# Edge counting in a graph network kernel: one-hot rows built as a product of two small one-hots, edge columns innermost

## The reference

```python
def step(h, _):
    messages = h[col] @ W_msg.T + b_msg                       # col = dst
    agg = jax.ops.segment_sum(messages, row, num_segments=num_nodes)   # row = src
    gi = agg @ W_ih.T + b_ih
    gh = h @ W_hh.T + b_hh
    r = sigmoid(i_r + h_r); z = sigmoid(i_z + h_z)
    n = tanh(i_n + r * h_n)
    return (1.0 - z) * n + z * h, None
h, _ = jax.lax.scan(step, x, None, length=5)
x = _layernorm(x + h)
```

## Time and profile before

| | us |
|---|---|
| median of 3 runs | 702.73 (701.65 to 703.63) |
| the profiled execution | 700.98 |
| its span, first to last instruction | 699.0 |

### The profile page before, as it was taken

How to read it: one execution, slowest core, us unless ns; L and a number is a source line. 1 busy time by engine, 2 the same in 40 slices (tenths; PEclk the granted TensorE clock), 3 DMA queues, 4 the chain that set the end, 5 groups by cost and what they waited for, 6 DMA issues and landing times.

```text
span 699.0 us, 8918 instructions
## 1 busy us (share of the span) xinstructions
PE 633.2 (91%) x3065; PEld 476.3 (68%) x3065; DVE 383.1 (55%) x1043; ACT 324.0 (46%) x557; POOL 261.3 (37%) x348
## 2 busy tenths in 40 slices
PE   3569888888899999999999999989999989999992
PEld 3445555555585587788778877867888868778861
DVE  4699999999966742332642223561332453244446
ACT  3446666666643443444444334433443443344342
POOL 6000000000012056566446655535676536556610
PEclk9579999999999999999999999999999999999997
DMA  5023333333300000000000000000000000000002
GB/s 162 23 59 83 83 87 89 87 87 87 86 25 0 0 1 1 0 1 0 1 1 1 0 1 0 1 0 1 1 0 1 1 0 1 1 0 1 0 21 74
DMA packets 37710, 18.71 MB, mean 27 GB/s; under 512 B 4588, under 2 KB 37482, under 8 KB 37662
## 3 DMA queue, kind: packets, MB, share of 16 engines
q1 hardware_dynamic: 35304, 16.70, 9.2%
q0 software_dynamic: 416, 0.83, 0.4%
q10 hardware_dynamic: 1942, 0.55, 0.3%
HBM read 2.96 MB, written 1.60 MB: 7 GB/s over the span
## 4 chain that ended last, share of the span: by engine, by line
PE 66%; DVE 28%; ACT 3%; issue 2%; DMA 1%; POOL 0%; DVEq 0%; ACTq 0%
PE PS L665 37%; DVE hot_row L1083 15%; PE PS L645 8%; PE PS L646 8%; DVE hot_key L1078 6%; PE PS L653 4%; PE PS L652 4%; PE PS L516 3%; PE PS L588 2%; ACT ring L872 1%; DVE parts L970 1%; DVE hT L1127 1%; DVE pre_n L1123 1%; DVE pre_n L1111 1%; ACT cand L865 1%
## 5 line engine op out<-in xcount | busy, mean ns | idle before, releaser
L480 POOL CAST ring<-A 128x896 fp32r<-128x896 uint8 (+4 forms) x324 | 249.9, 810 | 399.3 <-PE PS L665 207.9
L665 PE MATMUL PS<-ring,parts 128*128 128x448 f32 x1372 | 301.4, 374 | 1.9 <-ACT ring L872 1.9
L665 PEld LDWEIGHTS PS<-ring,parts 128*128 128x128 f32 x1372 | 254.3, 188 | 31.2 <-issue 11.8
L1111 DVE SCALAR_TENSOR_TENSOR pre_n<-PS,small,gate_r 128x448 f32<-128x448 f32 x35 | 23.9, 683 | 232.9 <-PE PS L653 232.7
L1083 DVE TENSOR_SCALAR hot_row<-iota_row,rowT,valT 128x132 bf16<-128x132 bf16 x492 | 119.3, 314 | 0.0
L872 ACT ACTIVATE ring<-A 128x896 fp32r<-128x896 uint8 (+4 forms) x144 | 106.1, 776 | 0.1
L579 PE MATMUL PS<-hot_row,hot_key 128*128 128x132 bf16 x588 | 72.7, 237 | 25.9 <-DVE hot_row L1083 25.3
L579 PEld LDWEIGHTS PS<-hot_row,hot_key 128*128 128x128 bf16 x588 | 45.8, 132 | 72.1 <-ACT stage L815 47.5
L855 ACT ACTIVATE gate_r<-PS,small 128x448 f32<-128x448 f32 x35 | 22.2, 634 | 155.4 <-PE PS L646 155.4
L588 PE MATMUL PS<-spread,parts 128*128 128x448 f32 x294 | 83.8, 396 | 0.0
L826 ACT ACTIVATE spread<-A 128x1056 fp32r<-128x1056 uint8 (+1 forms) x75 | 70.3, 943 | 2.5 <-DMA A<-stage 2.5
(11 more groups left out here) (113 smaller groups left out, 437.0 us busy)
## 6 DMA issues: line engine op xcount, KB each, us to landing
A<-stage SPq DMA_DIRECT2D x200, 66.0 KB, 2.5
y<-in_x SPq DMA_DIRECT2D x4, 384.0 KB, 5.0
out<-y SPq DMA_DIRECT2D x4, 192.0 KB, 2.4
out<-y SPq DMA_DIRECT2D x3, 256.0 KB, 2.3
w_raw<-in_L_gnn_W_ih ACTq DMA_DIRECT2D x1, 192.0 KB, 3.8
w_raw<-in_L_gnn_W_hh ACTq DMA_DIRECT2D x1, 192.0 KB, 5.3
w_raw<-in_L_gnn_W_msg ACTq DMA_DIRECT2D x1, 64.0 KB, 2.1
bmsg<-in_L_gnn_b_msg ACTq DMA_DIRECT2D x1, 64.0 KB, 4.8
```

The source lines that it names most:

```text
L480: last = nc.gpsimd.tensor_copy(to, data)
L665: mm = pe.matmul(PS[:, AGG_BANKS[(t * LEGS + b) % 2], 0:LW], parts[:, k, part, :], ring[:, SLOT_OF[at_piece] % SLOTS, k % 2, :], start=(k ...
```

## The change

The number of source words in a range, 132, is written as 6 times 22 (HIGH, LOW). The one-hot of a column becomes the product of a one-hot of its high part (6 places, multiplied with the value of the plane) and one of its low part (22 places). The small one-hots are made for four pairs at once, in two buffers; the large one is a single product for each pair. All have the column of edges innermost, with one place of padding, so that 12 bytes lie between neighbouring places of a row. PE reads the moving operand with this stride. The `count` of a pair waits once for the pair's one-hots, and no longer once for each side. The preparation computes low and high part in place of the column, makes the planes as integers in one DVE instruction (ACT makes a float copy), transposes four things in place of three, and the work on the keys is divided between ACT and DVE, with ACT's second pass over the keys ahead of its copies to `keyT`.

```diff
-            for i, slots in enumerate((plane, column, key)):
-                pe.wait_ge(slots_made, i + 1)
+            for i, slots in enumerate((plane, low, high, key)):
+                if i == PLANE_AT:
+                    pe.wait_ge(planes_kept, 1)
+                else:
+                    pe.wait_ge(slots_made, i)
+                if i == KEY_AT:
+                    pe.wait_ge(slots_kept, PLANE_AT + 1)
+                for bank, c in (tuple((SLOT_BANKS[i], c) for c in range(COLS)) if i < KEY_AT else
+                                tuple((KEY_BANKS[side], c) for side in range(SIDES) for c in COLS_OF[side])):
...
+                    pe.wait_ge(hots_ready, p + 1)
                     for side in sides(p):
-                        pe.wait_ge(hots_ready, hots(p, side))
                         for n, c in enumerate(COLS_OF[side]):
                             mm = pe.matmul(PS[:, COUNT_BANKS[p % 2], side * CW:(side + 1) * CW],
-                                           hot_key[:, p % HOTS, :, 3 * side + n], hot_row[:, p % HOTS, c, :],
+                                           hot_key[:, p % HOTS, :, 3 * side + n], hot_row[:, p % HOTS, :, c],
...
-            nc.gpsimd.iota(iota_row, ...)
+            for turned in (highT, lowT, valT):
+                last = nc.gpsimd.memset(turned[:, :, COLS:PLACES], 0.0)
+            nc.gpsimd.iota(iota_high ...)
+            nc.gpsimd.iota(iota_low ...)
...
-            link(nc.vector.tensor_scalar(planes, nodes, -(WORDS - 1) / 2, 1.0 / WORDS, ALU.add, ALU.mult))
-            nc.vector.tensor_scalar(planes, planes, ROUND, ROUND, ALU.add, ALU.subtract).then_inc(slots_made, 1)
+            nc.vector.tensor_scalar(planes, nodes, -(WORDS - 1) / 2, 1.0 / WORDS, ALU.add, ALU.mult).then_inc(planes_made, 1)
...
-            link(nc.vector.tensor_scalar(ranges, words, -(CW - 1) / 2, 1.0 / CW, ALU.add, ALU.mult))
-            nc.vector.scalar_tensor_tensor(out=columns, in0=ranges, scalar=-float(CW), in1=words,
+            link(nc.vector.tensor_scalar(all_lines, words, -(LOW - 1) / 2, 1.0 / LOW, ALU.add, ALU.mult))
+            nc.vector.scalar_tensor_tensor(out=low[0:PAIRS, :, :], in0=all_lines, scalar=-float(LOW), in1=words,
+                                           op0=ALU.mult, op1=ALU.add).then_inc(slots_made, 1)
+            link(nc.vector.tensor_scalar(ranges, all_lines, -(HIGH - 1) / 2, 1.0 / HIGH, ALU.add, ALU.mult))
+            nc.vector.scalar_tensor_tensor(out=high[0:PAIRS, :, :], in0=ranges, scalar=-float(HIGH), in1=all_lines,
...
+            def high_and_low(k):
+                nc.vector.tensor_tensor(hot_high[:, k % 2, :, :, :],
+                                        iota_high.unsqueeze(1).to_broadcast([P, PT, HIGH, PLACES]),
+                                        highT[:, pairs_of(k), :].unsqueeze(2).to_broadcast([P, PT, HIGH, PLACES]),
+                                        ALU.is_equal).then_inc(factors_made, 1)
+                nc.vector.tensor_tensor(hot_low[:, k % 2, :, :, :], ... [P, PT, LOW, PLACES] ..., ALU.is_equal)
+            def high_times_value(k):
+                dve.wait_ge(factors_made, 3 * k + 1)
+                nc.vector.tensor_tensor(hot_high[:, k % 2, :, :, :], hot_high[:, k % 2, :, :, :],
+                                        valT[:, pairs_of(k), :] ..., ALU.mult).then_inc(factors_made, 1)
...
                 def one_hots(p):
+                    k, q = divmod(p, PT)
                     if p >= HOTS:
                         dve.wait_ge(counted, p - HOTS + 1)
                     nc.vector.tensor_tensor(hot_key[:, p % HOTS, :, :], iota_key,
                                             keyT[:, p, :].unsqueeze(1).to_broadcast([P, P, KEYS]), ALU.is_equal)
-                    for side in sides(p):
-                        for c in (COLS_OF[0], COLS_OF[1][1:])[side]:
-                            n = c * PAIRS + p
-                            last = nc.vector.tensor_scalar(hot_row[:, p % HOTS, c, :], iota_row, rowT[:, n:n + 1],
-                                                           valT[:, n:n + 1], ALU.is_equal, ALU.mult)
-                        last.then_inc(hots_ready, 1)
+                    if q == 0:
+                        dve.wait_ge(factors_made, 3 * (k + 1))
+                    nc.vector.tensor_tensor(
+                        hot_row[:, p % HOTS, :, :].rearrange("p (a b) c -> p a b c", a=HIGH),
+                        hot_high[:, k % 2, q, :, :].unsqueeze(2).to_broadcast([P, HIGH, LOW, PLACES]),
+                        hot_low[:, k % 2, q, :, :].unsqueeze(1).to_broadcast([P, HIGH, LOW, PLACES]),
+                        ALU.mult).then_inc(hots_ready, 1)
+                    if k + 1 < KT and q == HOTS - 1:
+                        high_and_low(k + 1)
+                    if k + 1 < KT and q == PT - 1:
+                        high_times_value(k + 1)
```

More of the change, by code:

```diff
@@ L28 @@
 KEYS = 6
+HIGH, LOW = 6, 22
+PLACES = 6
 LEGS = 7
@@ L169, in gnn_kernel @@
         rstd = closing.next("rstd", [P, KT, 1], F32)
-        assert closing.offset <= apart.offset
-        prep = Row(KT * WORDS * 4 - 32 * 1024)
+        assert closing.offset <= AT_FIRST + NP * 4
+        prep = Row(KT * WORDS * 4 - 40 * 1024)
         w_raw = prep.next("w_raw", [P, 7, P], F32)
@@ L182, in gnn_kernel @@
         word = prep.next("word", [P, SIDES, WIN], F32)
+        whole_plane = prep.next("whole_plane", [P, SIDES, WIN], I32)
+        line = prep.next("line", [P, SIDES, WIN], I32)
         rng = prep.next("rng", [P, SIDES, WIN], I32)
-        column = prep.next("column", [P, SIDES, WIN], F32)
+        low = prep.next("low", [P, SIDES, WIN], F32)
+        high = prep.next("high", [P, SIDES, WIN], F32)
         key = prep.next("key", [P, SIDES, WIN], F32)
@@ L303, in sides @@
             return range(2 if p < FULL_PAIRS else 1)
-        def hots(p, side):
-            return (2 * p + side if p < FULL_PAIRS else FULL_PAIRS + p) + 1
+        PLANE_AT, LOW_AT, HIGH_AT, KEY_AT = range(4)
         def landed(k):
@@ L784, in _, with turned @@
                 high_part(0, u)
[L786 to L789, removed]
+            act.wait_ge(planes_made, 1)
+            nc.scalar.activation(plane[0:PAIRS, :, :], whole_plane[0:PAIRS, :, :], ACT.Copy).then_inc(planes_kept, 1)
+            def turned(bank):
+                return PS[:, bank, 0:COLS * PAIRS].rearrange("p (c n) -> p n c", c=COLS)
+            act.wait_ge(slots_turned, PLANE_AT + 1)
+            nc.scalar.activation(valT[:, :, 0:COLS], turned(SLOT_BANKS[PLANE_AT]), ACT.Exp, scale=LOG_256).then_inc(slots_kept, 1)
+            act.wait_ge(slots_turned, LOW_AT + 1)
+            nc.scalar.activation(lowT[:, :, 0:COLS], turned(SLOT_BANKS[LOW_AT]), ACT.Copy).then_inc(slots_kept, 1)
+            act.wait_ge(slots_turned, HIGH_AT + 1)
+            nc.scalar.activation(highT[:, :, 0:COLS], turned(SLOT_BANKS[HIGH_AT]), ACT.Copy).then_inc(slots_kept, 1)
             act.wait_ge(consts_made, 3)
-            act.wait_ge(slots_made, 3)
+            act.wait_ge(slots_made, KEY_AT)
             nc.scalar.activation(apart_key[0:PAIRS, :, :], key[0:PAIRS, :, :], ACT.Abs, bias=key_mid[0:PAIRS, :]).then_inc(distance_made, 1)
[L794 to L801, removed]
             act.wait_ge(distance_made, 1)
@@ L804, in _ @@
                                  accum_out=matched).then_inc(matched_made, 1)
+            act.wait_ge(keys_zeroed, 1)
+            act.wait_ge(slots_turned, KEY_AT + 1)
+            nc.scalar.activation(keyT[:, :, 0:2], turned(KEY_BANKS[0])[:, :, 0:2], ACT.Copy)
+            nc.scalar.activation(keyT[0:HALF, :, 2], turned(KEY_BANKS[0])[0:HALF, :, 2], ACT.Copy).then_inc(slots_kept, 1)
             act.wait_ge(flag_set, 1)
@@ L1044, in _ @@
             nodes, groups_dst = win_src[0:PAIRS, :, :], win_dst[0:PAIRS, :, :]
[L1045 removed]
+            planes, words, all_lines, ranges, keys = (t[0:PAIRS, :, :] for t in (whole_plane, word, line, rng, key))
             dve.wait_ge(src_in, 32)
[L1047 to L1049 removed]
+            nc.vector.tensor_scalar(planes, nodes, -(WORDS - 1) / 2, 1.0 / WORDS, ALU.add, ALU.mult).then_inc(planes_made, 1)
+            dve.wait_ge(planes_made, 1)
             link(nc.vector.scalar_tensor_tensor(out=words, in0=planes, scalar=-float(WORDS), in1=nodes, op0=ALU.mult, op1=ALU.add))
[L1051 to L1052 removed]
+            link(nc.vector.tensor_scalar(all_lines, words, -(LOW - 1) / 2, 1.0 / LOW, ALU.add, ALU.mult))
[3 more added lines that the diff above has]
+            nc.vector.scalar_tensor_tensor(out=high[0:PAIRS, :, :], in0=ranges, scalar=-float(HIGH), in1=all_lines,
                                            op0=ALU.mult, op1=ALU.add).then_inc(slots_made, 1)
```

60 lines of the change are left out of this document (45 added, 15 removed).

## The result

The changed kernel takes 710.4 us (median of 4 runs, 707.6 to 711.0) against 703.2 (701.7 to 703.8): a ratio of 1.010, 95% interval 1.0073 to 1.0126: a small loss, but the interval leaves out a ratio of one. Forecast were 676, with 667 to 691 as range. The forecast was wrong in sign; the mechanism that acted is that of the rival "slower than before".

What follows compares the result with a forecast made beforehand. DVE was taken to bound the counting, with SP next. Gains of 1.3 (start), 3.7 (first pairs), 21.2 (SP's pace) and 0.5 (tail) sum to 26.7 us: 700.98 to 674.3 profiled, 676 as median; range 667 to 691.

Steps and rivals of the forecast that it cites:

- slower than before: Rival in the counting: PE's strided reads at a factor of four, 2.03 us a pair, 740 us; chance 0.06.
- The stride of PE's moving operand: PE's count matmuls: 12 bytes between neighbours cost zero; each factor slower would cost 0.36 us a pair.
- The third rival: PE in the counting at a factor of four, 740 us, deciding from a factor of 2.8 on; chance 0.06.
- DVE: One-hots in the counting: DVE's pace falls from 1.59 to 1.11 us a pair; other end 1.65.
- SP as what is late next: From pair 11 on the counting settles at SP's DMA issues, 1.28 us a pair, gaining 21.2 us.
- The first eleven pairs: Start of the counting: eight pairs gain 0.46 to 0.48 us each, together 3.7 us.
- The preparation: Before the counting: first `hot_key` at 26.2, 1.1 us earlier, and first count 1.3 us earlier.
- POOL's cover: In the preparation: POOL's idle 1.00 us covers its added memsets and small iota; without it 0.5 us.
- One wait in place of two: PE's wait for a pair's one-hots in the counting: nothing for the steady stage.
- the moved buffers: They cost nothing, since their first users stand behind semaphores that are long past.
- A reading: Slices of the earlier profile: DVE at 9 tenths in ten slices from about 35 us on.

Runs made afterwards that it cites:

- the contiguous read: The changed kernel with PE's moving operand alone read as 132 neighbouring numbers, not every sixth (counts not the reference's): 674.4 us, ratio 0.961.
- halving SP's issues: The contiguous read with the second DMA of each pair issued by POOL in place of SP: 655.5 us, ratio 0.934.
- the single product: The changed kernel with its one product laid out with two columns of edges innermost, so PE reads 4 bytes apart: 676.7 us, ratio 0.964.

## Why the prediction was wrong

**The stride of PE's moving operand: the step that failed.** I took zero for it, from the weight loads. The term measured 6 x (0.179 - 0.059) = 0.72 us a pair: PE needs 1.70 in place of 0.95, which is over DVE's old 1.59 and SP's 1.28, so PE and not SP set the pace. The nearest row was of another kind of read, and it bound nothing. The measured price, in all seven reads, is

| bytes between neighbours | us from matmul to matmul | 16-byte lines touched by 132 columns | ns a line |
|---|---|---|---|
| 2 | 0.058 | 16.5 | - |
| 4 | 0.063 | 33 | 1.9 |
| 8 | 0.122 | 66 | 1.85 |
| 10 | 0.151 | 82.5 | 1.83 |
| 12 | 0.179 | 99 | 1.81 |
| 16 | 0.238 | 132 | 1.80 |
| 24 | 0.238 | 132 | 1.80 |

A line costs 1.8 ns, and a matmul about the larger of that sum and of its columns at the clock (132 at 2.4 GHz are 55 ns); the two cheapest reads, 0.058 and 0.063, lie 3 and 4 ns over this. The Trainium skill's "Advanced Engine Details and Errata", section SBUF Cachelines, has the 16-byte line, and the saturation agrees with it; its "at least two hits on a cacheline" does not suffice here: 8 bytes are two hits and cost double. The Trainium skill's "SBUF — State Buffer", section Door 1: The DMA port swizzle, says of the same lines that bf16 can stride by 8 numbers for free; read as a stride, by the runs 8 numbers, 16 bytes, cost four times the contiguous read.

**The third rival was right as a mechanism.** It said: PE in the counting, slower than before from a factor of 2.8 on. The factor is 3.0, and the result 7 us above before; its own price, 740 us, was for a factor of four, one fetch for each column. That is what the reads at 16 and 24 bytes show (0.238 = 4.0 x 0.059); at 12 bytes only 99 of 132 columns open a new line. Its sum at 3.0 gives 0.95 + 2 x 0.36 = 1.67 us a pair and, with 0.08 us on 88 pairs less 1.3, about 708 us. I gave it 0.06, because I let the weight loads speak against it twice, in the sum and in the chance. The text itself drew a bound from a factor of one to one of four, and the sum and the range took its lower part alone; what a page's rule says against a change, with no row of the same kind to contradict it, deserved more.

**DVE: right.** 1.11 us a pair forecast, 1.108 measured where nothing else binds. That the second repeated operand and the third dimension keep the fast rate was an assumption from `hot_key` and held: 0.564 us.

**SP as what is late next: right, once PE reads contiguously.** In the changed kernel itself SP waits 33.1 us of 130 for ACT's copies, behind PE. With the contiguous read SP's last issue starts at 170.0 us (about 170 forecast), its issues are 0.64 apart with the long ones at a mean of 0.678 (119.1/177 = 0.673 forecast), the gates start at 180.2 (181), and the time is 674.4 (676). The forecast was thus the time of the change without its stride; halving SP's issues showed that SP was the bound. That it met 674.4 so closely is in part luck, since errors cancel: from 200 issues of SP, the 23rd starts 5.1 us earlier than before (5.0 forecast), the stretch to the last is shortened by 20.3 (21.2), and the end behind it by 1.9 (0.5).

**The first eleven pairs: about right.** From the first `hot_key` to that of pair 11 the kernel before takes 24.7 us, the contiguous read 20.3, 4.4 less (3.7 forecast), the changed kernel 21.8.

**The preparation: mis-sized.** Forecast was the first `hot_key` at 26.2; it came at 27.1, 0.2 us earlier than before and not 1.1. POOL's cover was too thin. Its timeline after, as the earlier trace rows:

```profile
8.24 0.45 POOL L476 MEMSET highT<- 128x100 bf16 x1
8.36 0.67 POOL L476 MEMSET lowT<- 128x100 bf16 x1
8.70 0.67 POOL L476 MEMSET valT<- 128x100 bf16 x1
...
9.75 2.54 POOL L482 IOTA iota_key<- 128x768 bf16 x1
12.63 1.04 POOL L487 DMA_INDIRECT win_src<-in_src,small  x1 [0.34 <-DVE small L1074]
```

`iota_key` starts 1.55 us later than before, not 0.6, and ends at 12.29; the source windows are fetched 0.9 us later than before. In the chain of the changed kernel DVE's conversion of the starts lies between them:

```profile
11.60 0.73 DVE small L1074
```

It takes 0.72 us, where the same instruction took 0.17 before (at 11.27, with POOL done at 10.74), and it ends as `iota_key` does. So POOL seems to have held DVE up as well; no run separated this. The rest of the preparation is as worked out: the chain no longer waits for ACT's copies; the key's last instruction starts 4.8 us after the first pass over the windows (17.15 to 21.9), 0.7 more than before (16.31 to 20.33); and from that first pass to the first `hot_key` it is 9.9 us in place of 11.0, the 1.1 forecast. The late windows take 0.8 of them back.

**One wait in place of two: nothing, right.** For the moved buffers nothing was seen either, but no run separated them.

**A reading.** DVE stands at 9 tenths in nine slices of the earlier trace rows, not ten; nothing was worked out from it.

## What to carry to other kernels

A layout that saves one engine instructions hands its stride to the engine that reads it; before choosing it, count the 16-byte lines that a moving operand touches, at 1.8 ns each, against its columns at the clock. For bf16, two one-hots side by side, so that PE's numbers lie 4 bytes apart, cost next to nothing, and a repeated operand's dimensions can often be ordered so that one DVE instruction still makes such rows. A bound for an operation comes from a row of the same kind of read; where there is none, the unknown factor belongs in the range with the point from which it decides, and a chance that does not use the same indirect row twice. And when an engine's pace is cut, look at the issuing queues, which are in no busy share: here SP's 0.64 us for a DMA was the next bound, and a second queue was worth 19 us with the contiguous read and 21 with the single product.

## What the runs showed of the hardware

- A moving operand costs 1.8 ns for each 16-byte line that it touches, whatever PE's clock: in the changed kernel matmul to matmul is 0.179 us at the lower and at the upper level of the granted clock, and with 16 bytes 0.238 at both, whereas contiguous reads take 0.109 to 0.111 at the lower and 0.058 at the upper one.
- The same price would explain a row of before: 448 columns of four bytes lie on 112 lines, 0.202 us, and the earlier trace rows has 0.206 for a matmul, more than 448 columns at 2.4 GHz (0.187). By this estimate an operand of four bytes is at the edge even when it is contiguous; no run tested it.
- Weight loads 12 bytes apart show no such price: 2 ns from matmul to matmul, 9 ns in the duration of a load.
- The granted clock stood at the lower level with PE busy all the time by the profile: 0.50 over 60 us, with matmuls that were slowed to 0.238 us by their reads.
